# Graph attention and edge ordering: scores spread from two row halves, bf16 for zeros and ones, runs innermost and scans

## The chip, the cores and the metric

The kernel runs on one core of a Trainium2 chip. A core has a matrix engine (TensorE, PE in the profile, with its weight loads as PEld), a vector engine (VectorE, DVE), a scalar engine (ScalarE, ACT), GpSimd (POOL) and a sync engine (SP) that issues most DMAs. Each has its own instruction stream, and they wait for each other by semaphores. The metric is the device time of one execution, in microseconds (us).

## The reference

Two graph layers over 12,500 nodes and 200,000 edges sorted by destination. The change touches the first layer (attention) and the ordering of the edges that the second one (three graph convolutions) needs.

```python
h = jnp.maximum(_layernorm(x, axis=-1), 0.0)
# attention, 8 heads of 16
q, k, v = ((h @ W.T).reshape(N, 8, 16) for W in (Wq, Wk, Wv))
scores = jnp.einsum('ehc,ehc->eh', q[dst], k[src]) / np.sqrt(16) + edge_attr @ We.T
seg_max = jax.ops.segment_max(scores, dst, num_segments=N)
ex = jnp.exp(scores - seg_max[dst])
denom = jax.ops.segment_sum(ex, dst, num_segments=N)
out = jax.ops.segment_sum(v[src] * (ex / denom[dst])[:, :, None], dst, num_segments=N)
x = x + out.reshape(N, 128)
h = jnp.maximum(_layernorm(x, axis=-1), 0.0)
# three times: (h @ W)[src] * norm summed over dst, bias, ReLU, batch norm
x = x + gcn3(h)
```

## The kernel before

**Attention** (`attend`) takes the edges in 196 blocks of 1024, eight chunks of 128 lanes each. For one block GpSimd gathers the rows of k and v (`gather`, line 740, eight indirect DMAs), SyncE loads the queries and edge features. TensorE turns one-hot tables of the lanes (`hot`) and of the block's nodes (`place`) round (`turn_hot`, `turn_place`, lines 1000 and 1004), spreads the queries over the edges (`spread_q`, line 949, in two halves of the array's rows), and adds the bias (`bias`, line 1013). VectorE multiplies and adds up (`products`, `add_up`, `add_bias`); the 64 scores of a lane are turned (`turn_scores`, line 969), copied by ScalarE into `sct`, and spread over two PSUM banks (`spread_scores`, line 989, eight f32 matmuls from 64 rows, on top of a mask that `mask`, line 974, has put there). VectorE takes the two maxima (`run_max`, line 795). `near_max` (lines 926, 928, 930) brings the maxima to the nodes, `raise_max` compares with the running maximum, `scale_exp` on ScalarE makes the factor by which older sums shrink, `spread_scale` (lines 914 and 915) spreads it for the numerators and the denominators, and `shrink` and `merge` apply it on VectorE. `messages` weights v by the exponentials, `sum_up` (line 906) sums the messages by lane, and `put_nodes` (lines 937, 938) puts them to the nodes.

`steps` sets the order: each engine has a list of (lag, step). In turn i of the loop an engine does the steps of its list in that order, each on block i minus its lag. So the list is the engine's queue, and blocks i to i-4 are under way at once. The loop's body holds four turns.

**Edge ordering** (`rank`) takes 50 spans of 28 columns by 128 edges. VectorE makes a one-hot of each edge's tile (`tile_hot`, line 1651, 3584 elements), halves it by adding (`halve`, line 1659) and sums over columns in five doubling adds (`add_up`, line 1676); TensorE counts earlier equal edges (`match`, lines 1810 and 1815, with ScalarE's ReLU behind each of seven batches, then `add_ranks`). From the rank VectorE decides the slot, numbers the edges that do not fit by five more doubling adds (`run_up`, line 1702), makes one-hots of the slot's line (`line_hot`, line 1777, 28 operations) and chunk (`chunk_hot`, line 1754), loads the payload (`load_pay`, line 1763), and TensorE puts the payload down with 28 matmuls (`put_down`, line 1845). Columns are the outer dimension of these tables, the 128 lines or 29 chunks the inner one. Lags run from 0 to 4 here too, with two turns in the body.

The lines on which the order rests:

```python
for k in range(slots):
    for lag, stage in stages:
        stage(step(t * slots + (k - lag), (k - lag) % slots, t + (k - lag) // slots))
```

## Time and profile before

| | |
|---|---|
| median of 3 runs (lowest, highest) | 6932.62 us (6927.31, 6932.69) |
| the profiled execution | 6936.31 us, span 6934.5 us |
| busy share of TensorE, VectorE, ScalarE, GpSimd | 83%, 67%, 31%, 45% |
| attention, first gather to last | 219.8 to 3072.7 us |
| ordering, first to last one-hot of a tile | 3324.8 to 4010.9 us |

A busy share over the whole span mixes stages with different limits, so it is read by stage. In the rows a group is one source line on one engine; "x16" counts the instructions that a row merges, the first number is the start, the second how long the row lasts, and what stands in brackets is how long the engine was idle before it and what ended that. An f32 matmul leaves two records, a bf16 matmul or an f32 transpose one. Busy times of TensorE can touch although the engine waits a little, since the ends of its matmuls are modelled.

### The profile page before, as it was taken

To read this page: it belongs to the slowest core of one execution; us is meant where nothing else is said; L and a number is where in the kernel's file an instruction comes from. 1 tells how busy PE (TensorE), PEld (TensorE's weight loads), DVE (VectorE), ACT (ScalarE), POOL (GpSimd) and SP (SyncE) were. 2 spreads that over 40 slices of the span, in tenths; PEclk is the share of its full clock that TensorE was granted. 3 is DMA by queue.
4 is the path that set the end of the run, shared out by engine and by line. 5 is a ranking of instruction groups with operands and counts; after the bars stand their busy time and mean duration, and the time that the engine had idled before them with its cause. 6 is when DMAs were issued, how large, how long until landed. Compare 5 with 4: busy or idle time off the path is not lost. (4 is left out here: it accounts for less than half of the span.)

```text
span 6934.5 us, 161023 instructions
## 1 busy us (share of the span) xinstructions
...
## 2 busy tenths in 40 slices
...
PEclk9655555555555555555556679999999999799997
...
GB/s 145 116 89 87 88 87 88 88 88 89 87 87 87 88 89 86 89 70 131 86 66 70 65 115 105 106 103 104 102 128 104 104 105 101 163 104 106 106 102 152
DMA packets 542000, 688.39 MB, mean 99 GB/s; under 512 B 217072, under 2 KB 427905, under 8 KB 541722
## 3 DMA queue, kind: packets, MB, share of 16 engines
...
q1 hardware_dynamic: 401692, 348.45, 16.6%
...
## 5 line engine op out<-in xcount | busy, mean ns | idle before, releaser
L740 POOL DMA_INDIRECT at_kv<-kv_tab,at_idx x1568 | 1562.2, 996 | 1296.6 <-issue 593.6
L2250 ACT ACTIVATE ag_msg<-ag_pair 128x768 bf16<-128x768 f32 x1200 | 925.9, 808 | 1586.4 <-PE ag_pair L2180 1027.1
L2189 PE MATMUL ag_sum<-ag_hot,ag_msg 128*128 128x240 bf16 x10800 | 1300.5, 268 | 69.6 <-issue 55.5
L2189 PEld LDWEIGHTS ag_sum<-ag_hot,ag_msg 128*128 128x128 bf16 x10800 | 974.6, 98 | 443.3 <-issue 366.6
L2064 POOL DMA_INDIRECT ag_spill<-g_tab,ag_idx x600 | 580.1, 967 | 1429.5 <-DMA ag_idx<-spill_tab 777.8
L2119 DVE CAST ag_msg<-ag_pair 128x768 bf16<-128x768 f32 x600 | 572.9, 955 | 588.8 <-PE ag_pair L2180 277.2
L2180 PE MATMUL ag_pair<-xs,ag_pick 128*32 128x384 bf16 x14400 | 821.3, 331 | 153.4 <-DVE ag_pick L2092 63.0
L2071 POOL DMA_INDIRECT ag_spill<-g_tab,ag_idx x750 | 724.5, 966 | 462.3 <-issue 179.1
L2102 DVE TENSOR_SCALAR ag_hot<-iota_win,ag_node 128x240 bf16<-128x240 bf16 x4350 | 901.2, 290 | 0.0
L989 PE MATMUL at_ps_bc<-at_sct,at_sel_head 64*128 64x128 f32 x3136 | 696.8, 408 | 33.9 <-issue 8.2
L989 PEld LDWEIGHTS at_ps_bc<-at_sct,at_sel_head 64*128 64x128 f32 x3136 | 639.2, 308 | 52.0 <-ACT at_sct L1059 41.1
L2180 PEld LDWEIGHTS ag_pair<-xs,ag_pick 128*32 128x32 bf16 x14400 | 305.9, 95 | 476.1 <-issue 251.3
L795 DVE TENSOR_REDUCE at_ml<-at_ps_bc 128x4 f32<-128x512 f32 x392 | 267.6, 690 | 388.3 <-issue 201.4
L1810 PE MATMUL rk_t<-ar_later,ar_negi 128*128 128x512 bf16 x350 | 202.3, 578 | 179.9 <-DVE rk_oht L1651 178.6
L1073 ACT ACTIVATE at_hot_b<-at_ps_turn 128x128 bf16<-128x128 f32 x196 | 54.3, 277 | 891.4 <-PE at_ps_turn L1004 603.7
L1867 ACT ACTIVATE rk_tm<-rk_t 128x512 bf16<-128x512 f32 x350 | 208.4, 597 | 292.3 <-PE rk_t L1815 290.5
L2092 DVE TENSOR_SCALAR ag_pick<-ag_pick,iota_p 128x1024 bf16<-128x1024 bf16 x450 | 217.4, 483 | 101.9 <-DMA ag_pick<-slot_tab 94.2
L776 DVE TENSOR_TENSOR at_prod<-at_ps_q,at_kv 128x512 f32<-128x512 f32 x392 | 252.4, 686 | 48.9 <-issue 30.5
L1045 ACT ACTIVATE at_fall<-at_drop 8x128 f32<-8x128 f32 x196 | 60.5, 309 | 703.9 <-DVE at_drop L845 639.0
L949 PE MATMUL at_ps_q<-at_qd,at_hot_b 64*128 64x512 bf16 x1176 | 253.7, 558 | 12.4 <-DVE at_prod L776 7.7
L2189 PE MATMUL ag_sum<-ag_hot,ag_spill 128*128 128x240 bf16 x2250 | 256.7, 266 | 2.5 <-issue 2.4
L1777 DVE TENSOR_SCALAR rk_ohw<-ar_iota_col,rk_line_f 128x128 bf16<-128x128 bf16 x1400 | 256.4, 246 | 0.0
...
## 6 DMA issues: line engine op xcount, KB each, us to landing
...
at_attr<-attr SPq DMA_DIRECT2D x196, 128.0 KB
at_qd<-q_tab SPq DMA_DIRECT2D x1568, 12.0 KB
at_kv<-kv_tab,at_idx POOLq DMA_INDIRECT x1568
...
```

Of the source, the lines that this page charges most:

```text
L740: nc.gpsimd.indirect_dma_start(kv[:, s.slot, ch, :], None, env["kv_tab"], bass.IndirectOffsetOnAxis(ap=idx[:, s.slot, ch:ch + 1], axis=0)) ...
L795: nc.vector.tensor_reduce(ml[:, HALF * j:HALF * (j + 1)], ps_bc[j][:, :].rearrange("p (h e) -> p h e", e=P), AX.X, ALU.max).then_inc(bc_re ...
L949: last = nc.tensor.matmul(ps_q[j][:, :].rearrange("p (c d) -> p c d", d=DIM), hot_b[own, k, :], qd[own, k % 2, HALF * j:HALF * (j + 1), pa ...
L989: last = nc.tensor.matmul(ps_bc[j][:, h * P:(h + 1) * P], sel_head[:, HALF * j + h, :], sct[:, s.slot % 2, :], start=False, stop=h == HALF ...
L1777: last = nc.vector.tensor_scalar(ohw[:, s.slot, ch, :], iota_col[:, :], line_f[:, s.slot, ch:ch + 1], None, ALU.is_equal)
L2064: nc.gpsimd.indirect_dma_start(spill[:, k, o, :], None, table, bass.IndirectOffsetOnAxis(ap=idx[:, k, o:o + 1], axis=0)).then_inc(tail_in[ ...
L2071: nc.gpsimd.indirect_dma_start(spill[:, k, o, :], None, table, bass.IndirectOffsetOnAxis(ap=idx[:, k, o:o + 1], axis=0)).then_inc(spill_in ...
L2102: last = nc.vector.tensor_scalar(hot[:, k, ch, :], env["iota_win"][:, :], node[:, k, ch:ch + 1], None, ALU.is_equal)
L2119: nc.vector.tensor_copy(msg[:, p % 4, :, :], pair_ps[p % 3][:, :, 0:3 * DIM]).then_inc(copied[p], 1)
L2180: last = nc.tensor.matmul(pair_ps[p % 3][at, ch % 2, 0:3 * DIM], pick[:, k, ch * P + j * CAP:ch * P + (j + 1) * CAP], xs[:, (P // CAP) * c ...
L2189: last = nc.tensor.matmul(sum_ps[k][:, 0:WIN], row[:, part * DIM:(part + 1) * DIM], hot[:, k, ch, :], start=first and part == 0, stop=end ...
L2250: nc.scalar.activation(msg[:, p % 4, :, :], pair_ps[p % 3][:, :, 0:3 * DIM], ACT.Copy).then_inc(copied[p], 1)
```

## The change

In attention: `turn_scores` writes the 64 turned scores twice, to PSUM rows 0 to 63 and 64 to 127, with two f32 matmuls against the identity side by side; `sct` and `sel_head` get 128 rows; `spread_scores` is one step in which each head of the first bank (lower 64 rows) is followed by one of the second (upper 64 rows). The one-hot `hot`, a copy of `place` that ScalarE makes (`cast_place`), the identity, and the constants of the first two `near_max` matmuls are bf16. The turning of the two one-hots is a bf16 matmul. The matmul with `sel_aux` is gone: ScalarE makes the denominators' factor with a second exponential into `scale_d`, which `shrink` reads. TensorE sums the messages after turning the one-hots, and VectorE makes `place` and `hot` before the messages.

In the ordering: the tables `ohc`, `ohw`, `pay` have the 28 columns innermost; `line_hot` is four tensor_tensor of 32 lines by 28 columns against a constant `iota_x`; the two chains of doubling adds are each one scan; the matmuls of `put_down` read their operands with a step of 28 elements; VectorE's list is shorter and in another order.

```diff
-        sel_head = tile("sel_head", [C * HEADS, HEADS, P])
+        sel_head = tile("sel_head", [P, HALF, P])
...
-        big_c = tile("big_c", [P, HEADS, C])
-        low_row = tile("low_row", [1, HEADS * C])
-        ones_row = tile("ones_row", [1, P])
+        ident16 = tile("ident16", [P, P], BF16)
+        big_c = tile("big_c", [P, HEADS, C], BF16)
+        low_row = tile("low_row", [1, HEADS * C], BF16)
+        ones_row = tile("ones_row", [1, P], BF16)
...
-        hot = tile("hot", [P, SLOTS, P])
+        hot = tile("hot", [P, SLOTS, P], BF16)
+        place_b = tile("place_b", [P, SLOTS, P], BF16)
-        sct = tile("sct", [C * HEADS, 2, P])
+        sct = tile("sct", [P, 2, P])
...
+        scale_d = tile("scale_d", [P, P])
...
+                    dve.wait_ge(den_scale_made, s.nth)
-                    nc.vector.tensor_tensor(den, den, sa_ps, ALU.mult).then_inc(scaled, 1)
+                    nc.vector.tensor_tensor(den, den, scale_d[AUXD:AUXROWS, :], ALU.mult).then_inc(scaled, 1)
...
                     pe.wait_ge(above_made, s.nth if isinstance(s.n, int) and s.n == sh.BLOCKS - 1 else s.nth + 1)
-                    nc.tensor.matmul(sf_ps, sel_feat[:, :, :].rearrange("h d e -> h (d e)"), scale[0:HEADS, :], start=True, stop=True)
-                    nc.tensor.matmul(sa_ps, sel_aux[:, :], scale[:, :], start=True, stop=True,
-                                     tile_position=(0, AUXD)).then_inc(scale_spread, 1)
+                    nc.tensor.matmul(sf_ps, sel_feat[:, :, :].rearrange("h d e -> h (d e)"), scale[:, :], start=True,
+                                     stop=True).then_inc(scale_spread, 1)
 
                 def spread_max(s):
                     pe.wait_ge(md_made, s.nth)
...
+                    pe.wait_ge(place_cast, s.nth)
...
-                    nc.tensor.matmul(near_ps, place[:, s.slot, :], big_c[:, :, :], start=False, stop=False,
+                    nc.tensor.matmul(near_ps, place_b[:, s.slot, :], big_c[:, :, :], start=False, stop=False,
                     nc.tensor.matmul(near_ps, place[:, s.slot, :], md[:, :, :].rearrange("p c h -> p h c"),
...
-                    nc.tensor.transpose(sct_ps, sc[:, s.slot, :], ident[:, :]).then_inc(sc_turned, 1)
+                    for j in range(2):
+                        at = slice(C * HEADS * j, C * HEADS * (j + 1))
+                        last = nc.tensor.matmul(sct_ps[at, :], sc[:, s.slot, :], ident[:, :], start=True, stop=True,
+                                                tile_position=(0, C * HEADS * j))
+                    last.then_inc(sc_turned, 1)
...
-                def spread_scores(j):
-                    def run(s):
-                        pe.wait_ge(sct_made, s.nth)
-                        for h in range(HALF):
-                            last = nc.tensor.matmul(ps_bc[j][:, h * P:(h + 1) * P], sel_head[:, HALF * j + h, :],
-                                                    sct[:, s.slot % 2, :], start=False, stop=h == HALF - 1,
-                                                    skip_group_check=True)
-                        last.then_inc(bc_made[j], 1)
-                    return run
+                def spread_scores(s):
+                    pe.wait_ge(sct_made, s.nth)
+                    for h in range(HALF):
+                        for j in range(2):
+                            own = slice(C * HEADS * j, C * HEADS * (j + 1))
+                            last = nc.tensor.matmul(ps_bc[j][:, h * P:(h + 1) * P], sel_head[own, h, :],
+                                                    sct[own, s.slot % 2, :], start=False, stop=h == HALF - 1,
+                                                    skip_group_check=True, tile_position=(C * HEADS * j, 0))
+                            if h == HALF - 1:
+                                last.then_inc(bc_made[j], 1)
-                    nc.tensor.transpose(hot_ps, hot[:, s.slot, :], ident[:, :]).then_inc(hot_turned, 1)
+                    nc.tensor.matmul(hot_ps, hot[:, s.slot, :], ident16[:, :], start=True, stop=True).then_inc(hot_turned, 1)
-                    pe.wait_ge(place_made, s.nth)
-                    nc.tensor.transpose(place_ps, place[:, s.slot, :], ident[:, :]).then_inc(place_turned, 1)
+                    pe.wait_ge(place_cast, s.nth)
+                    nc.tensor.matmul(place_ps, place_b[:, s.slot, :], ident16[:, :], start=True, stop=True
+                                     ).then_inc(place_turned, 1)
...
-                    (2, spread_scores(0)), (2, spread_scores(1)), (3, sum_up), (0, turn_hot), (0, turn_place)], w)
+                    (2, spread_scores), (0, turn_hot), (0, turn_place), (3, sum_up)], w)
...
-                    nc.scalar.activation(scale[0:HEADS, :], fall[:, :], ACT.Exp, bias=env["zero_t"][0:HEADS, :],
+                    nc.scalar.activation(scale[:, :], fall[:, :], ACT.Exp, bias=env["zero_t"][0:HEADS, :],
...
+                    nc.scalar.activation(scale_d[AUXD:AUXD + HEADS, :], fall[:, :], ACT.Exp,
+                                         bias=env["zero_t"][0:HEADS, :], scale=-1.0).then_inc(den_scale_made, 1)
...
+                def cast_place(s):
+                    act.wait_ge(place_made, s.nth)
+                    nc.scalar.activation(place_b[:, s.slot, :], place[:, s.slot, :], ACT.Copy).then_inc(place_cast, 1)
+
...
-        ohc = tile("ohc", [P, SPAN_C, PLACE_C], BF16)
-        ohw = tile("ohw", [P, 2, SPAN_C, P], BF16)
-        pay = tile("pay", [P, 2, SPAN_C, PAY], BF16)
...
+        ohc = tile("ohc", [P, PLACE_C, SPAN_C], BF16)
+        ohw = tile("ohw", [P, 2, P, SPAN_C], BF16)
+        pay = tile("pay", [P, 2, PAY, SPAN_C], BF16)
...
+            nc.gpsimd.iota(iota_x[:, :, :], pattern=[[1, P], [0, SPAN_C]], base=0, channel_multiplier=0,
...
-                to = sums[0][:, PAD + 1:PAD + SPAN_C].unsqueeze(2)
-                nc.vector.tensor_tensor(to, halves[5][:, 0:SPAN_C - 1, 0:1], halves[5][:, 0:SPAN_C - 1, 1:2], ALU.add
-                                        ).then_inc(summed[0], 1)
-
-            def add_up(k):
-                def go(s):
-                    dve.wait_ge(summed[k - 1], s.nth)
-                    v, d = sums[k - 1], 1 << (k - 1)
-                    if k == 5:
-                        s.freed(dve, ranked, 2)
-                    to = before_c[:, s.slot, :] if k == 5 else sums[k][:, PAD:PAD + SPAN_C]
-                    op = nc.vector.tensor_tensor(to, v[:, PAD:PAD + SPAN_C], v[:, PAD - d:PAD - d + SPAN_C], ALU.add)
...
-                return go
+                s.freed(dve, ranked, 2)
+                nc.vector.tensor_tensor_scan(before_c[:, s.slot, 1:SPAN_C], halves[5][:, 0:SPAN_C - 1, 0],
+                                             halves[5][:, 0:SPAN_C - 1, 1], 0.0, ALU.add, ALU.add
+                                             ).then_inc(half_made, 1)
...
-            def run_up(k):
-                def go(s):
-                    dve.wait_ge(spill_made if k == 1 else run[k - 2], s.nth)
-                    v, d = spills[k - 1], 1 << (k - 1)
-                    n = SPAN_C + 1
-                    nc.vector.tensor_tensor(spills[k][:, PAD:PAD + n], v[:, PAD:PAD + n], v[:, PAD - d:PAD - d + n],
-                                            ALU.add).then_inc(run[k - 1], 1)
-                return go
+            def run_up(s):
+                dve.wait_ge(spill_made, s.nth)
+                s.freed(dve, over_made, 1)
+                nc.vector.tensor_tensor_scan(queue[:, 1:SPAN_C + 1], spills[:, :], none[:, :], 0.0, ALU.add, ALU.add
+                                             ).then_inc(queued, 1)
...
-                nc.vector.tensor_tensor(ohc[:, :, :], chunk_f[:, :].unsqueeze(2).to_broadcast([P, SPAN_C, PLACE_C]),
-                                        iota_chunk[:, :].unsqueeze(1).to_broadcast([P, SPAN_C, PLACE_C]),
-                                        ALU.is_equal).then_inc(ohc_made, 1)
+                nc.vector.tensor_tensor(ohc[:, :, :], chunk_f[:, :].unsqueeze(1).to_broadcast([P, PLACE_C, SPAN_C]),
+                                        iota_x[:, 0:PLACE_C, :], ALU.is_equal).then_inc(ohc_made, 1)
-                nc.vector.tensor_tensor(pay[:, k, :, 0:2 * PLACE_C].rearrange("p c (v m) -> p v c m", v=2),
-                                        ohc[:, :, :].unsqueeze(1).to_broadcast([P, 2, SPAN_C, PLACE_C]),
-                                        kept["vals"][:, :, here(s)].unsqueeze(3).to_broadcast(
-                                            [P, 2, SPAN_C, PLACE_C]), ALU.mult).then_inc(pay_made, 1)
...
+                nc.vector.tensor_tensor(pay[:, k, 0:2 * PLACE_C, :].rearrange("p (v m) c -> p v m c", v=2),
+                                        ohc[:, :, :].unsqueeze(1).to_broadcast([P, 2, PLACE_C, SPAN_C]),
+                                        kept["vals"][:, :, here(s)].unsqueeze(2).to_broadcast(
+                                            [P, 2, PLACE_C, SPAN_C]), ALU.mult).then_inc(pay_made, 1)
...
-                    for ch in range(q * 4, q * 4 + 4):
-                        last = nc.vector.tensor_scalar(ohw[:, s.slot, ch, :], iota_col[:, :],
-                                                       line_f[:, s.slot, ch:ch + 1], None, ALU.is_equal)
-                    if q == 6:
-                        last.then_inc(ohw_made, 1)
+                    at = slice(q * P // 4, (q + 1) * P // 4)
+                    op = nc.vector.tensor_tensor(ohw[:, s.slot, at, :], line_f[:, s.slot, :].unsqueeze(1).to_broadcast(
+                        [P, P // 4, SPAN_C]), iota_x[:, at, :], ALU.is_equal)
+                    if q == 3:
+                        op.then_inc(ohw_made, 1)
...
-                    last = nc.tensor.matmul(p_ps[k][:, 0:PAY], ohw[:, k, ch, :], pay[:, k, ch, :], start=ch == 0,
+                    last = nc.tensor.matmul(p_ps[k][:, 0:PAY], ohw[:, k, :, ch], pay[:, k, :, ch], start=ch == 0,
```

On TensorE, the middle of a turn of the attention loop before: turn_max, turn_scores, give_back, spread_scores, the sum (906), the two turns.

```order
L963 MATMUL at_ps_max<-ident,at_mnew 128x8
L966 REGISTER_ALU
L967 REGISTER_ALU
L969 MATMUL at_ps_turn<-ident,at_sc 64x128
L982 MATMUL at_ps_max<-at_m_node,at_place_t 128x8
L989 MATMUL at_ps_bc<-at_sct,at_sel_head 128x128 x8
L902 REGISTER_ALU
L906 MATMUL at_ps_node<-at_msg,at_hot_w 32x137 x8
L996 ISA
L82 REGISTER_ALU
L1000 MATMUL at_ps_turn<-ident,at_hot 128x128
L1004 MATMUL at_ps_turn<-ident,at_place 128x128
```

The same place now (999 is the spread, 911 the sum):

```order
L976 MATMUL at_ps_turn<-ident,at_sc 64x128 x2
L991 MATMUL at_ps_max<-at_m_node,at_place_t 128x8
L999 MATMUL at_ps_bc<-at_sct,at_sel_head 128x128 x8
L1006 ISA
L82 REGISTER_ALU
L1010 MATMUL at_ps_turn<-at_ident,at_hot 128x128
L1014 MATMUL at_ps_turn<-at_ident,at_place_b 128x128
L907 REGISTER_ALU
L911 MATMUL at_ps_node<-at_msg,at_hot_w 32x137 x8
L983 MATMUL at_ps_bc<-at_miss_b,at_identb 128x512 x2
```

The scores are turned by two matmuls instead of one, the spread still has eight, and the sum stands behind the two turns.

On VectorE, the end of that turn before: the bias added (789), the merge (879, 880), messages (817), short (853), hot, place, and the next turn's maxima (795).

```order
L789 TENSOR_TENSOR at_sc<-at_qk,at_ps_scale 128x64
L876 REGISTER_ALU
L879 TENSOR_TENSOR state<-state,at_ps_node 128x128
L880 TENSOR_TENSOR aux<-aux,at_ps_node 9x128
L817 TENSOR_TENSOR at_msg<-at_kv,at_msg 128x8x128
L853 TENSOR_TENSOR at_short<-at_ps_max,at_ml 128x8
L82 ISA
L758 ISA
L758 TENSOR_TENSOR at_hot<-rel,iota_w 128x128
L766 ISA
L766 TENSOR_TENSOR at_place<-off,iota_n 128x128
L795 TENSOR_REDUCE at_ml<-at_ps_bc 128x4 x2
```

And now (793 adds the bias, 821 is the messages, 799 the maxima):

```order
L884 TENSOR_TENSOR state<-state,at_ps_node 128x128
L885 TENSOR_TENSOR aux<-aux,at_ps_node 9x128
L82 ISA
L770 ISA
L770 TENSOR_TENSOR at_place<-off,iota_n 128x128
L762 ISA
L762 TENSOR_TENSOR at_hot<-rel,iota_w 128x128
L821 TENSOR_TENSOR at_msg<-at_kv,at_msg 128x8x128
L857 TENSOR_TENSOR at_short<-at_ps_max,at_ml 128x8
L799 TENSOR_REDUCE at_ml<-at_ps_bc 128x4 x2
```

`place` and `hot` moved ahead of the messages; the count of operations is the same.

On VectorE in the ordering loop before: the small tiles' halvings between adds, from the second halving to the second group of one-hot lines.

```order
L1659 TENSOR_TENSOR rk_half<-rk_half 128x896
L1702 TENSOR_TENSOR rk_spills<-rk_spills 128x29
L1659 TENSOR_TENSOR rk_half<-rk_half 128x448
L1702 TENSOR_TENSOR rk_spills<-rk_spills 128x29
L1659 TENSOR_TENSOR rk_half<-rk_half 128x224
L1702 TENSOR_TENSOR rk_spills<-rk_spills 128x29
L1659 TENSOR_TENSOR rk_half<-rk_half 128x112
L1702 TENSOR_TENSOR rk_spills<-rk_spills 128x29
L1659 TENSOR_TENSOR rk_half<-rk_half 128x56
L1708 CAST rk_spill_n<-rk_spills 128x1
L1666 TENSOR_TENSOR rk_sums<-rk_half 128x27
L1777 TENSOR_SCALAR rk_ohw<-ar_iota_col,rk_line_f 128x128 x4
```

And now, from the same halving (1783 is a quarter of the one-hot lines, 1685 the scan of the running count):

```order
L1678 TENSOR_TENSOR rk_half<-rk_half 128x896
L1715 CAST rk_spill_n<-rk_queue 128x1
L1678 TENSOR_TENSOR rk_half<-rk_half 128x448
L1783 TENSOR_TENSOR rk_ohw<-rk_line_f,rk_iota_x 128x896
L1678 TENSOR_TENSOR rk_half<-rk_half 128x224
L1678 TENSOR_TENSOR rk_half<-rk_half 128x112
L1719 TENSOR_SCALAR rk_over<-rk_queue,rk_ahead 128x28
L1678 TENSOR_TENSOR rk_half<-rk_half 128x56
L1725 TENSOR_TENSOR rk_diff<-rk_place,rk_over 128x28
L1685 SCALAR_TENSOR_TENSOR rk_before_c<-rk_half 128x27
```

The adds over spills (1702) are gone from between the halvings, where one scan (1709, ahead of these rows) does their work, and the groups of four one-hot lines have become one operation of 896 elements.

## Rows read from the trace of the kernel before

**Rows 1.** The page: busy time and share of the span; granted clock in 40 slices.
```profile
span 6934.5 us, 161023 instructions
...
PEclk9655555555555555555556679999999999799997
```

**Rows 2.** Stretches: us, busy time by engine (instructions), granted clock, DMA share, GB/s.
```profile
1000.00:2000.00 1000.00, 920.19 (x4573) 637.59 (x4571) 578.01 (x1433) 227.87 (x952) 543.33 (x546) 0.57 0.31 88
3320.00:3610.00 290.00, 189.18 (x2467) 130.91 (x2468) 276.15 (x1319) 101.85 (x221) 0.84 (x11) 0.61 0.24 72
```

**Rows 3.** Line 989: times run, ns min/median/max, first and last start.
```profile
L989 PE MATMUL at_ps_bc<-at_sct,at_sel_head x3136: 272/417/579, 237.3 to 3097.2; 64*128 64x128 f32 x196
```

**Rows 4.** TensorE in one block: start us, us, line, operation, count, idle before.
```profile
2982.80 3.78 PE L989 MATMUL at_ps_bc<-at_sct,at_sel_head 64*128 64x128 f32 x16
2986.50 1.16 PE L906 MATMUL at_ps_node<-at_msg,at_hot_w 128*32 128x137 f32 x16
...
2988.08 1.06 PE L974 MATMUL at_ps_bc<-at_miss_b,at_identb 128*128 128x512 bf16 x2
...
2989.39 0.69 PE L926 MATMUL at_ps_max<-at_low_row,at_ones_row 1*128 1x64 f32 x2
2990.00 0.69 PE L928 MATMUL at_ps_max<-at_big_c,at_place 128*128 128x64 f32 x2
2990.48 0.63 PE L930 MATMUL at_ps_max<-at_md,at_place 128*128 128x64 f32 x2
...
2991.77 0.59 PE L915 MATMUL at_ps_scale<-at_scale,at_sel_aux 9*9 9x128 f32 x2
2992.29 0.79 PE L937 MATMUL at_ps_node<-at_place,at_nodes 128*128 128x128 f32 x2
...
2993.85 1.46 PE L949 MATMUL at_ps_q<-at_qd,at_hot_b 64*128 64x512 bf16 x6
...
2996.88 0.40 PE L969 MATMUL at_ps_turn<-ident,at_sc 128*64 128x128 f32 x1 [0.37 <-DVE at_sc L789]
...
2997.71 3.78 PE L989 MATMUL at_ps_bc<-at_sct,at_sel_head 64*128 64x128 f32 x16
```

**Rows 5.** The same line 989, one block later and the next.
```profile
3012.63 3.78 PE L989 MATMUL at_ps_bc<-at_sct,at_sel_head 64*128 64x128 f32 x16
...
3024.55 2.47 PE L989 MATMUL at_ps_bc<-at_sct,at_sel_head 64*128 64x128 f32 x16 [0.18 <-ACT at_sct L1059]
```

**Rows 6.** A stretch of that block.
```profile
3020.00:3022.00 2.00, 2.00 (x14) 1.08 (x14) 1.55 (x3) 0.35 (x2) 1.34 (x2) 1.00 0.36 111
```

**Rows 7.** VectorE around the loop's edge: start us, us, line, count, idle before.
```profile
3028.75 1.29 DVE L795 TENSOR_REDUCE at_ml<-at_ps_bc 128x4 f32<-128x512 f32 x2 [2.72 <-remote]
```

**Rows 8.** The page: the gathers on GpSimd, busy us, mean ns, idle before.
```profile
L740 POOL DMA_INDIRECT at_kv<-kv_tab,at_idx x1568 | 1562.2, 996 | 1296.6 <-issue 593.6
```

**Rows 9.** VectorE in one span of the ordering stage.
```profile
3699.78 1.08 DVE L1659 TENSOR_TENSOR rk_half<-rk_oht 128x1792 bf16<-128x1792 bf16 x1
3700.78 0.18 DVE L1702 TENSOR_TENSOR rk_spills<-rk_spills 128x29 f32<-128x29 f32 x1
3700.89 0.62 DVE L1659 TENSOR_TENSOR rk_half<-rk_half 128x896 bf16<-128x896 bf16 x1
...
3702.86 0.73 DVE L1777 TENSOR_SCALAR rk_ohw<-ar_iota_col,rk_line_f 128x128 bf16<-128x128 bf16 x4
...
3708.72 0.99 DVE L1754 TENSOR_TENSOR rk_ohc<-rk_chunk_f,ar_iota_chunk 128x812 bf16<-128x812 bf16 x1
3709.93 1.85 DVE L1763 TENSOR_TENSOR rk_pay<-rk_ohc,ar_vals 128x1624 bf16<-128x1624 bf16 x1 [0.21 <-DVE rk_ohc L1754]
...
3714.00 1.08 DVE L1659 TENSOR_TENSOR rk_half<-rk_oht 128x1792 bf16<-128x1792 bf16 x1
```

**Rows 10.** TensorE in the same span.
```profile
3709.05 1.65 PE L1845 MATMUL rk_p<-rk_pay,rk_ohw 128*128 128x63 bf16 x28 [2.18 <-DVE rk_ohw L1777]
3713.21 0.61 PE L1810 MATMUL rk_t<-ar_later,ar_negi 128*128 128x512 bf16 x1 [2.51 <-DVE rk_oht L1651]
```

92 lines of the change are left out of this document (46 added, 46 removed).

## Prediction

> **What bounds the kernel now.** I read the page first, then a table by stages, then the order of time inside one turn of each loop that the change touches. One core runs for 6934.5 us, 6936.31 with what lies around the span; the median of the three runs is 6932.62, so the profiled run stands 3.7 us above it [rows 1]. The change touches two stages. Attention runs from about 220 to 3100 us in 196 blocks; the edge ordering from about 3325 to 4040 us in 50 spans. The rest (3 layers of aggregation, where the clock is high) is not touched, and I leave it at its time.
>
> In attention TensorE is busy 92% of a stretch of 1000 us, VectorE 58%, ScalarE 23%, GpSimd 54%, and the granted clock is 0.57, so it is mostly the lower level, 1.2 GHz [rows 2]. From the first to the last start of line 989, less the 3.3 us inside the last block, a block takes (3097.2 - 237.3 - 3.3) / 195 = 14.65 us [rows 3]. One block at 1.2 GHz goes from 2982.80 to 2997.71, 14.91 us, and TensorE's starts follow each other nearly without a gap: the waits there are 0.37 us for the scores and some tenths before line 989 [rows 4]. Here TensorE is the bound, and time taken out of its chain comes off the block.
>
> In the ordering the picture turns round. VectorE is busy 276.15 of 290 us, 95%, TensorE 65%, ScalarE 35% [rows 2]. A span takes 3714.00 - 3699.78 = 14.22 us [rows 9]; TensorE waits 2.18 us in it for the one-hot lines and 2.51 us for the next tile's one-hot [rows 10]. VectorE is the bound.
>
> **Attention, part by part (at 1.2 GHz).**
> (a) The spread of scores: eight f32 matmuls, 16 records, take 2986.50 - 2982.80 = 3.70 us, of which 0.35 is the change-over to the next line's tiling (16 steps of 0.21 are 3.35) [rows 4]. Each uses 64 of the 128 rows. Afterwards they go in four pairs, one of the lower half of the rows and one of the upper. Line 949 already does that, in bf16: six matmuls of 128x512 in 1.46 us. Two full-height ones of the same size (line 974) take 1.06, with one inside them 0.63 long, thus 0.43 apart; six in a row would take 5 x 0.43 + 0.63 = 2.8. So the halves there run side by side [rows 4]. If f32 does the same, 3.35 becomes 1.7 and the term is -1.65. The other bound: the f32 weights are loaded one after the other, and as 16 loads fill the 3.35 us as well as the matmuls do, nothing is gained: 0. I take -1.65, by line 949.
> (b) The matmul of line 915 goes: 2992.29 - 2991.77 = -0.52 [rows 4]. In its place ScalarE makes a second exponential and VectorE reads it from SBUF; ScalarE is at 23%.
> (c) Lines 926 and 928 become bf16, one record instead of two: now 0.61 + 0.48 = 1.09 us [rows 4]. Half is -0.5; bounds -0.2 (only the second record's step) and -0.8. The bf16 copy of place is one more ScalarE step of some 0.3 us, which TensorE meets only in turn_place, over 1.5 us later.
> (d) turn_hot and turn_place remain one record each: 0.
> (e) turn_scores (line 969, one record of 0.40) becomes two f32 matmuls side by side with two records each: one step of 0.21 more, and it lies on the path from scores to spread. +0.24.
> (f) Moving the sum behind the two transposes changes no amount of work. On VectorE place and hot now stand before the messages, so the sum's input is 0.5 us later, but the two transposes now cover that: 0.
> Sum: -1.65 - 0.52 - 0.5 + 0.24 = -2.43, about -2.5 with the gaps; 14.91 becomes 12.4.
>
> What is late next? Both halves of the spread now end together, so VectorE has its two maxima (1.29 us for two, rows 7) wholly behind it, where one lay beside the second half before. TensorE has the transposes (0.5), the sum (1.1) and the first mask (0.4) to do meanwhile: the cover is 2.0 us against 1.5, just enough. Around the edge of the loop, once in four blocks, VectorE comes 2.72 us late with these maxima [rows 7]; today the second half of the spread and the rest hide about half of that, afterwards less: +0.7 us in four blocks, 0.2 a block. GpSimd needs (1562.2 + 593.6) / 196 = 11.0 us a block for eight gathers and the gaps that nothing explains [rows 8]: a floor at 11.0, not at 12.4. VectorE has 0.58 x 14.65 = 8.5 us.
>
> The clock: the block that begins at 3012.63 takes 11.92 us (next start 3024.55), with the clock at 1.00 in a stretch of it [rows 5, 6]. It rises there right behind the sum, the transposes and the two masks. The mean of 14.65 against the cold block's 14.91 says that rises less edge stalls give 0.26 a block. That run of work stays and comes round more often, so I expect somewhat more: a net 0.5 with the edge taken off. Block: 12.4 - 0.5 = 11.9 us. Gain 2.75 x 195 = 536 us; from the bounds of (a), (c) and the clock, between 190 and 712 (the floor of 11.0).
>
> **Ordering, part by part.**
> (g) One-hot lines: 28 tensor_scalar of 128x128, four in 0.73 us, 0.65 from start to start: 7 x 0.65 = 4.55 us. Now four tensor_tensor of 128x896 bf16 with unit step inside. The row of that size, line 1659, has the next start 0.54 later when one small operation of 0.11 lies between; I take 0.54 each, 2.16. -2.4 [rows 9].
> (h) load_pay: 1.85 us for 1624 elements with a broadcast innermost; 1792 elements with unit steps take 1.08. -0.9. chunk_hot: 0.99 for 812 against 0.62 for 896. -0.4 [rows 9]. Bound for (g) and (h): if a broadcast in the middle keeps the slow rate, 1.85 us per 1624, then (g) is 4.0 and (h) nothing.
> (i) Five adds for the running count, five for the spills, 0.11 each from start to start [rows 9], become one scan each. The trace has no scan; between 0.1 and 0.5 us each for 28 elements. I take 0.2: -0.7, bounds -0.9 and -0.1.
> (j) With fewer fillers the last steps follow each other: +0.3 (line 1763 waits 0.21 on its neighbour now).
> Sum: -4.1, 14.22 becomes 10.1 on VectorE.
> (k) TensorE's put_down, 28 matmuls in 1.65 us [rows 10], now reads weights and payload with a step of 28 elements, 56 bytes. The trace has no bf16 operand so; line 930 reads f32 with a step of 32 bytes and takes 0.63 where line 928 with unit step takes 0.69 [rows 4], so at that step nothing shows beside the weight load. Line 989 streams 128 columns in 0.21 us a record, so line 930's 64 would take 0.11 and could take up to 0.21, twice as long, unseen behind its weights. Bounds: 1.65 and, if each load of 128 columns goes as slowly as f32 weights do (0.21), 28 x 0.21 = 6 us. TensorE's turn is 14.22 less its waits 2.18 and 2.51 and the some 1.1 for the spill count: 8.4 with put_down at 1.65, so it carries up to 3.3 before it binds at 10.1, and at 6 us a span takes 12.8. I take 3.3, the twofold that line 930 allows, and with the change-overs 10.5 us a span.
> The Trainium skill speaks against this part: its page "SBUF — State Buffer", section "Door 1: The DMA port swizzle", note on cachelines, says that every access which moves to another 16-byte line pays, so that bf16 is free only up to a step of 8 elements. Line 930 steps over two lines each time and shows no penalty, or one hidden behind its weights; at 28 elements no run shows it yet. By that page put_down would cost more than 1.65, by line 930 alone 1.65, and the span 10.5 or 10.1.
> Gain 3.7 x 50 = 185 us, between 70 and 230. The constants of this stage (a larger iota) are made while VectorE waits for the first load: nothing.
>
> Sum: 6936.3 - 536 - 185 = 6215, and 3.7 less against the median: 6212, say 6210.
>
> **Rivals.**
> High clock: TensorE is at 2.4 GHz so much that attention comes to GpSimd's 11.0 us. For it: block 3012.63 shows 11.92 even before the change. Against: the mean clock of 0.57 says that it falls back each time [rows 2]. 6936 - 712 - 185 = 6040.
> The halves do not overlap in f32: (a) is 0, block 13.6 us, gain 205: 6936 - 205 - 185 = 6546. Against it stands line 949, for it only that its weights are bf16.
> Ordering keeps its time: the broadcast stays slow, or the strided loads cost 6 us, gain some 70: 6330.
> Slower: changing between the row halves empties the array as changing the tiling does, 0.35 us each time. Seven changes inside the spread cost 2.45 instead of -1.65: the block is 14.91 + 2.45 - 0.78 = 16.6 or, with the clock, 16.3, +320 us; with the ordering's -185: 7070. It decides from some 0.2 us for each change. Line 949, which changes five times in 1.46 us, is against it. The Trainium skill has the same distinction: "TensorEngine Tiling (Array Packing)", section on key properties, says that changing the tiling mode drains the engine and that tiles of one mode run in parallel. By that this rival costs nothing; the 0.35 behind line 989, a change of mode, agrees.
>
> **Chances.** Both parts work, about 6210 (own range 6080 to 6350): 0.68. High clock, 6040: 0.10. No overlap, 6546: 0.07. Ordering keeps its time, 6330: 0.10. Slower, 7070: 0.05. The range 6060 to 6450 leaves out the no-overlap and slower cases and part of the high clock. A difference of 0.2% (14 us) is what can be told from none. Faster 0.94, same 0.01, slower 0.05.
>
> **What would show it.** In the changed profile: the 16 records of the spread within some 2.0 us instead of 3.78; a block at 12 us between starts; TensorE's waits in it still below 1 us, else another engine has taken over; VectorE's two maxima back to back, directly behind the spread. In the ordering: 896-element rows of some 0.6 us, the payload at 1.0, put_down's 28 matmuls in 2 to 4 us, a span at 10.5, VectorE over 90% busy. The forecast is wrong if the spread stays over 3 us, if a scan takes more than 0.5, or if TensorE waits for neither VectorE nor ScalarE in the ordering, which would mean that put_down binds.

## The result, and the profile after

The changed kernel takes 6664.91 us (6652.28 to 6674.67, 4 runs) against 6931.14: a ratio of 0.9616, interval 0.9598 to 0.9633. It is 266 us faster where 721 were forecast, and outside the forecast's range. The profiled run took 6652.28 us. In attention a block went from 14.65 to 14.18 us.

From the page of the kernel after (compare [rows 1]), then the table by stretches, whose columns are those of [rows 2]:

```profile
span 6650.5 us, 159851 instructions
...
PEclk9655555555555555555677699999999999899997
```

```profile
1000.00:2000.00 1000.00, 803.31 (x4677) 498.36 (x4673) 585.88 (x1485) 282.95 (x1133) 578.92 (x567) 0.56 0.33 91
3320.00:3610.00 290.00, 282.31 (x3418) 219.99 (x3416) 268.44 (x966) 134.40 (x315) 0.00 (x0) 0.75 0.31 91
```

The ordering did what was forecast. The 50 one-hots of a tile (line 1670 now) start within 498.4 us, 10.17 us a span; before, 3324.8 to 4010.9 makes 14.00. The line's row, and one span on VectorE and then on TensorE (answers to [rows 9, 10]):

```profile
L1670 DVE TENSOR_SCALAR rk_oht<-rk_hi_bc,iota_p x50: 1141/1144/1153, 3237.1 to 3735.5; 128x3584 bf16<-128x3584 bf16 x50
```

```profile
3508.29 0.58 DVE L1761 TENSOR_TENSOR rk_ohc<-rk_chunk_f,rk_iota_x 128x812 bf16<-128x812 bf16 x1
3509.09 1.00 DVE L1769 TENSOR_TENSOR rk_pay<-rk_ohc,ar_vals 128x1624 bf16<-128x1624 bf16 x1 [0.22 <-DVE rk_ohc L1761]
...
3511.49 0.62 DVE L1783 TENSOR_TENSOR rk_ohw<-rk_line_f,rk_iota_x 128x896 bf16<-128x896 bf16 x1
...
3513.12 0.21 DVE L1709 TENSOR_TENSOR_SCAN rk_queue<-rk_spills,rk_none 128x28 f32<-128x28 f32 x1
```

```profile
3508.91 3.43 PE L1849 MATMUL rk_p<-rk_pay,rk_ohw 128*128 128x63 bf16 x28
```

In attention TensorE's work shrank as forecast, yet it now stands idle: busy 803 of 1000 us instead of 920. The groups of TensorE in one block (answers to [rows 4]), and where VectorE waits:

```profile
1528.83 2.08 PE L999 MATMUL at_ps_bc<-at_sct,at_sel_head 64*128 64x128 f32 x16
1530.84 0.29 PE L1010 MATMUL at_ps_turn<-at_ident,at_hot 128*128 128x128 bf16 x1
1530.93 0.31 PE L1014 MATMUL at_ps_turn<-at_ident,at_place_b 128*128 128x128 bf16 x1
```

```profile
1528.01 1.02 POOL L744 DMA_INDIRECT at_kv<-kv_tab,at_idx  x1 [2.76 <-DVE aux L885]
1529.33 1.03 POOL L744 DMA_INDIRECT at_kv<-kv_tab,at_idx  x1 [0.30 <-issue]
1530.67 0.95 POOL L744 DMA_INDIRECT at_kv<-kv_tab,at_idx  x1 [0.30 <-issue]
...
1532.37 1.29 DVE L799 TENSOR_REDUCE at_ml<-at_ps_bc 128x4 f32<-128x512 f32 x2 [2.64 <-PE at_ps_bc L999]
...
1532.54 0.28 ACT L1088 ACTIVATE at_hot_b<-at_ps_turn 128x128 bf16<-128x128 f32 x1 [2.23 <-PE at_ps_turn L1014]
```

The spread is done at 1530.91, but VectorE's maxima, which need nothing else, begin at 1532.37; the two turned one-hots are done at 1531.24 and ScalarE starts on them at 1532.54. TensorE has worked, and nobody hears of it for 1.3 to 1.5 us. Three gathers started within the last 3 us. VectorE's waits over the same 1000 us (engine, waiting group, what ended the wait, us in total, times, longest):

```profile
DVE at_sc L793 <- remote: 100.0, 29, 3.6
DVE at_ml L799 <- PE at_ps_bc L999: 78.5, 38, 2.7
DVE at_mnew L848 <- remote: 33.5, 16, 2.7
```

"Remote" stands where no instruction ended shortly before the wait's end: the signal came long after its maker. The trace also holds when each semaphore was raised. Set against the ends of the matmuls that raise them (from 1000 to 2400 us), 54.5% of TensorE's updates come over 0.5 us late in the kernel after, 21% in the kernel before; of VectorE's and ScalarE's, none to speak of (0.02 and 0.03 us on average). By the number of gathers started in the 3.75 us before the end of the matmul (400 to 3000 us), over 0.3 us late are: with one 1% before and 2% after, with two 12% and 45%, with three 61% and 86%. The gathers themselves moved together: the median distance from one to the next is 1.61 us before and 1.27 after, and three in 3.75 us stand ahead of 27% of the matmuls' ends before and of 46% after (1000 to 2400 us). The trace of these runs lacks about half of all update records (of TensorE's in this stretch 21% before and 27% after); a missing one leads to the next block's, some 14 us off, which I left out. So the shares are those of the updates that were recorded.

### The profile page after: what moved, and what is told of

The parts are those of the page before. It is cut to its first block and busy times, and to the rows that moved or that the text cites. A ratio compares the mean times of both kernels' runs of the same rounds, so it can differ in the third digit from the quotient of the medians.

```text
span 6650.5 us, 159851 instructions
## 1 busy us (share of the span) xinstructions
PE 5406.7 (81%) x49582; PEld 3559.8 (54%) x49582; DVE 4418.8 (66%) x13500; ACT 2281.1 (34%) x5686; POOL 3152.5 (47%) x3144
## 3 DMA queue, kind: packets, MB, share of 16 engines
q0 software_dynamic: 140208, 338.71, 18.3%
## 5 line engine op out<-in xcount | busy, mean ns | idle before, releaser
L744 POOL DMA_INDIRECT at_kv<-kv_tab,at_idx x1568 | 1605.2, 1024 | 1169.3 <-issue 491.3
L799 DVE TENSOR_REDUCE at_ml<-at_ps_bc 128x4 f32<-128x512 f32 x392 | 252.8, 686 | 362.0 <-PE at_ps_bc L999 229.8
L999 PE MATMUL at_ps_bc<-at_sct,at_sel_head 64*128 64x128 f32 x3136 | 407.6, 438 | 11.4 <-issue 11.4
L999 PEld LDWEIGHTS at_ps_bc<-at_sct,at_sel_head 64*128 64x128 f32 x3136 | 350.0, 325 | 16.8 <-issue 12.1
L976 PE MATMUL at_ps_turn<-ident,at_sc 128*64 128x128 f32 x784 | 136.1, 440 | 242.9 <-DVE at_sc L793 227.6
L954 PE MATMUL at_ps_q<-at_qd,at_hot_b 64*128 64x512 bf16 x1176 | 283.7, 616 | 12.2 <-issue 7.1
L1024 PEld LDWEIGHTS at_ps_scale<-at_we,at_attr 128*128 128x128 f32 x784 | 181.1, 321 | 166.9 <-issue 99.3
L793 DVE TENSOR_TENSOR at_sc<-at_qk,at_ps_scale 128x64 f32<-128x64 f32 x196 | 42.6, 217 | 340.0 <-remote 281.2
L983 PE MATMUL at_ps_bc<-at_miss_b,at_identb 128*128 128x512 bf16 x392 | 194.9, 554 | 80.5 <-DVE at_ml L799 80.3
```

What stands on the lines that cost most here:

```text
L744: nc.gpsimd.indirect_dma_start(kv[:, s.slot, ch, :], None, env["kv_tab"], bass.IndirectOffsetOnAxis(ap=idx[:, s.slot, ch:ch + 1], axis=0)) ...
L799: nc.vector.tensor_reduce(ml[:, HALF * j:HALF * (j + 1)], ps_bc[j][:, :].rearrange("p (h e) -> p h e", e=P), AX.X, ALU.max).then_inc(bc_re ...
L954: last = nc.tensor.matmul(ps_q[j][:, :].rearrange("p (c d) -> p c d", d=DIM), hot_b[own, k, :], qd[own, k % 2, HALF * j:HALF * (j + 1), pa ...
L999: last = nc.tensor.matmul(ps_bc[j][:, h * P:(h + 1) * P], sel_head[own, h, :], sct[own, s.slot % 2, :], start=False, stop=h == HALF - 1, s ...
```

## The experiments

They ran in five sets, each on one chip, with the kernel before beside them. Kernels with plain loads or with half of the gathers do not compute the reference's values; all others do. The sets are of two kinds, and this turned out to be the heart of the case. In three (and in the first comparison) the kernel before took 6873 to 6931 us and TensorE's updates were late; I call them late sets. In two it took 6258 and 6264 us and no update was more than 0.30 us late; I call them prompt sets. Which kind a set would be could not be chosen, and it isn't simply the chip: the first prompt set and the first late one both ran on the chip with the number 2. Two kernels of different late sets are compared by their ratios, and the changed kernel itself had 0.9586 and 0.9616 there, so less than 0.003 between such ratios says nothing. Block is the mean time of a block in attention (the column of the late sets leaves out the first comparison).

| kernel | late sets: ratio, block | prompt sets: ratio, block |
|---|---|---|
| before | 1, 14.45 | 1, 12.5 (no trace of its own; from the last two rows) |
| after | 0.9586, 14.00 | 0.9206, 10.96 |
| ordering alone | 0.9718, 14.52 | |
| after, spread not in halves | 0.9454, 13.62 | 0.9421, 11.65 |
| after, two gates moved | 0.9519, 13.82 | 0.9196 and 0.9195, 10.97 and 11.04 |
| after, both of these | 0.9729, 14.61 | |
| after, a pause behind each gather | 0.9470, 13.66 | |
| after, plain loads for gathers | 0.8706, 10.93 | |
| after, half of them plain | 0.8680, 10.94 | |
| after, four gathers only | | 0.9156, 10.66 |
| before, one gate | 1.0937, 17.87 | 1.0006 and 1.0004, 12.52 and 12.56 |
| before, plain loads | | 0.9998, 12.54 |

**1. Half of the gathers.**

```diff
-                    for ch in range(C):
+                    for ch in range(0, C, 2):
                         pace(s, ch)
...
-                        for ch in range(HALF * j, HALF * (j + 1)):
+                        for ch in range(HALF * j, HALF * (j + 1), 2):
                             dve.wait_ge(kv_in[k][ch], 16 * s.use)
```

> The changed kernel with only four of the eight gathers of a block (chunks 0, 2, 4, 6; the rows of the other four chunks are left out, so half of the keys and values are zeros). Theory S (late signals): TensorE's semaphore updates reach the other engines 1 to 2 us late whenever GpSimd's gathers follow each other closely; in the changed kernel 45% of the updates with two gathers started in the last 3.75 us and 86% of those with three are over 0.3 us late. With half of the gathers nearly all come in time, and a block takes what TensorE's cold work needs, 12.5 us, or less, instead of 14.18: 6665 - 196 x (1.7 to 2.2), 6230 to 6330 us. Rival C (chain): with TensorE's work cut, the loop is held by a chain through VectorE and ScalarE that has nothing to do with gathers: 6640 to 6690 us. Rival K (clock): the missing gain is the clock that no longer rises; gathers do not matter for it either: 6640 to 6690 us.

It fell in a prompt set: 5725.2 us, ratio 0.9156 (0.9140 to 0.9173). Beside the changed kernel's 0.9206 in the other prompt set this says only that there four of the gathers and their data cost 0.3 us a block. The time expected was for a late set, so it decides nothing on the theory.

**2. The kernel before with one gate.** GpSimd waits ahead of each of the eight gathers for a step of VectorE (`pace`), which keeps them apart.

```diff
                 def pace(s, ch):
                     if ch == 0:
                         s.freed(pool, bc_read[0], 3)
-                    if ch == 1:
-                        s.freed(pool, md_made, 3)
...
```

> The kernel before, with seven of the eight gates in front of its gathers taken away (the first stays): the same eight gathers of a block start one behind the other. Theory S: they then stand 1.25 us apart over 10 of the 14.65 us, TensorE's signals come late as in the changed kernel, and the kernel before loses 0.5 to 1.5 us a block: 7030 to 7230 us. Rivals C and K: the gathers' places change nothing, the data only come earlier: 6920 to 6945 us.

Prompt set: 6256.97 us, 1.0006 (0.9993 to 1.0020). Repeated:

> The kernel before with only the first of its eight gates, run again because its first run fell in a set without late signals, where it changed nothing (ratio 1.0006). With late signals: the gathers stand 1.25 us apart through most of a block, over half of TensorE's updates are late, and the kernel before gets 100 to 300 us slower, ratio 1.015 to 1.045. A rival by which only the number of gathers in a block counts, and not how close they stand, has 0.997 to 1.003.

Again a prompt set: 6263.0 us, 1.0004 (0.9991 to 1.0017). And a third time:

> The kernel before with only the first of its eight gates. Its two runs so far fell in sets without late signals and changed nothing (1.0006, 1.0004). If this set has late signals: if closeness counts, more of TensorE's updates are late and it is 100 to 300 us slower, ratio 1.015 to 1.045; if only the number of gathers in a block counts, 0.997 to 1.003. Without late signals: 0.998 to 1.002 again.

This one was a late set, and the effect is over twice the most that I gave it: 7525.1 us, 1.0937 (1.0918 to 1.0955). The eight gathers in a row, and VectorE beside them:

```profile
1501.89 0.94 POOL L726 DMA_INDIRECT at_kv<-kv_tab,at_idx  x1 [8.65 <-DVE at_ml L781]
1503.14 0.95 POOL L726 DMA_INDIRECT at_kv<-kv_tab,at_idx  x1 [0.30 <-issue]
...
1510.64 0.95 POOL L726 DMA_INDIRECT at_kv<-kv_tab,at_idx  x1 [0.30 <-issue]
1519.17 0.94 POOL L726 DMA_INDIRECT at_kv<-kv_tab,at_idx  x1 [7.58 <-DVE at_ml L781]
```

```profile
1506.30 0.30 DVE L846 TENSOR_TENSOR at_nodes<-at_ps_node,at_gain 128x136 f32<-128x136 f32 x1
1510.42 0.23 DVE L810 TENSOR_REDUCE at_top_n<-at_ps_max 128x8 f32<-128x64 f32 x1 [3.81 <-remote]
```

The same work and the same number of gathers, only closer: 3.4 us more a block. Over half of the updates (56%) are over 0.5 us late, and a block that runs wholly at 1.2 GHz takes 18.3 us (median) where it takes 14.91 in a prompt set. In a prompt set the same edit does nothing. So in a late set it matters how close the gathers stand, with their number the same.

**3. Two gates moved in the kernel after.**

```diff
                     if ch == 3:
-                        s.freed(pool, near_read, 3)
+                        s.freed(pool, qk_made, 2)
                     if ch == 4:
-                        s.freed(pool, qk_made, 2)
+                        s.freed(pool, q_spread, 1)
```

The fourth gather now waits for another step of VectorE, the fifth for one of TensorE.

> The changed kernel with two gates of its gathers moved (the fourth gather waits for the sum of the products instead of the maxima at the nodes, the fifth for the queries' spread instead of the sum), so that the eight stand more evenly in a block. Theory S: fewer signals are late, but eight gathers in 12.5 us are still two to three in 3.75 us: 6520 to 6650 us. Rivals C and K: 6650 to 6680 us.

Prompt set: 5753.62 us, 0.9196 (0.9176 to 0.9217). Again, with the changed kernel beside it:

> The changed kernel with the gates of the fourth and fifth gather moved, run beside the changed kernel itself. With late signals: fewer of TensorE's updates fall behind a third gather, 20 to 150 us less than the changed kernel. Without late signals: within 20 us of the changed kernel.

Prompt set: 5764.74 us, 0.9195 (0.9176 to 0.9214), the same as the changed kernel's 5763.87. And in a late set:

> The changed kernel with the gates of the fourth and fifth gather moved. Without late signals it is the same as the changed kernel (0.9196 and 0.9195 against 0.9206). With late signals: 20 to 150 us less than the changed kernel, ratio 0.937 to 0.956; a rival by which eight gathers in a block make the same share of updates late wherever they stand has 0.956 to 0.962.

6549.42 us, 0.9519 (0.9503 to 0.9535) against the changed kernel's 0.9586 (0.9566 to 0.9606) in another late set: 36 us less by the times, 46 by the ratios. The share of late updates hardly moved (52% in both), so the share alone does not set the time. The trace shows TensorE busy 862 us of the stretch from 1000 to 2000 instead of 800, but at a clock of 0.52 instead of 0.57; which of the signals are late now was not worked out.

**4. The kernel after, as it is,** to have it in each kind of set.

> The changed kernel, unaltered. The four kernels run so far ran on another chip than the first comparison: there the kernel before takes 6258 us instead of 6931 and no semaphore update of TensorE is late in its trace, whether gathers stand close or not. Theory S' (the late signals belong to the first chip, and they are what held the change back there): on a chip without late signals the changed kernel gains more, ratio 0.91 to 0.925 (near the 0.9196 of the kernel with moved gates), on one with late signals 0.96 again. Rival: the ratio is 0.96 on every chip, and the moved gates alone brought the rest: 0.955 to 0.965.

Late set: 6585.86 us, 0.9586 (0.9566 to 0.9606).

> The changed kernel, unaltered, as the reference of this set. With late signals (the kernel before at 6870 to 6930 us): ratio 0.955 to 0.965. Without (the kernel before at some 6260): S' says 0.91 to 0.925.

Prompt set: 5763.87 us, 0.9206 (0.9191 to 0.9222), as the theory S' of the expectations had it. VectorE's waits there and the table of the stretch:

```profile
DVE at_sc L793 <- PE at_ps_scale L1024: 89.8, 82, 1.4
DVE at_ml L799 <- PE at_ps_bc L999: 67.4, 61, 1.1
```

```profile
1000.00:2000.00 1000.00, 897.31 (x6076) 565.39 (x6074) 754.84 (x1933) 363.98 (x1472) 749.49 (x737) 0.69 0.43 118
```

"Remote" is gone from the waits, no wait is over 1.4 us, and the clock is 0.69 instead of 0.56, although gathers start every 1.25 us.

**5. The kernel before, for its trace.**

> The kernel before, unaltered, for its trace beside the others. S': where it takes some 6260 us, no update of TensorE is late, cold blocks still take 14.9 us, and the clock is at 2.4 GHz for more than half of the blocks; where it takes some 6930, about a fifth of the updates is late.

Late set, 6865.95 us; 18% of the updates over 0.5 us late.

**6. The ordering alone.** `attend` as before, `rank` as after.

> Only the part of the change in the edge ordering; attention as before. A span went from 14.22 to 10.2 us in the first traces, so 50 x 4.0 = 200 us less whatever the chip: 6931 - 200 = 6730 or 6258 - 200 = 6058 us, ratio 0.968 to 0.971. A rival by which the faster ordering is given back elsewhere (code loading, the constants) has less than 150 us.

6676.23 us, 0.9718 (0.9699 to 0.9738): 197 us. In that set attention's part of the change is worth 6676 - 6586 = 90 us.

**7. Plain loads for gathers, in the kernel after.**

```diff
-                        nc.gpsimd.indirect_dma_start(
-                            kv[:, s.slot, ch, :], None, env["kv_tab"],
-                            bass.IndirectOffsetOnAxis(ap=idx[:, s.slot, ch:ch + 1], axis=0)
-                        ).then_inc(kv_in[s.slot][ch], 16)
+                        nc.gpsimd.dma_start(kv[:, s.slot, ch, :], env["kv_tab"][P * ch:P * (ch + 1), :]
+                                            ).then_inc(kv_in[s.slot][ch], 16)
```

> The changed kernel with the eight gathers of a block replaced by eight plain loads of the same bytes (128 rows of kv_tab in a row each, the same ones in every block; the data are not the edges'), issued by GpSimd at the same gates. On a chip with late signals: if it is the gather's work of making 128 descriptors that delays TensorE's signals, they come in time and the time falls by 350 us or more against the changed kernel; if it is the bytes, it stays within 50 us. On a chip without late signals: GpSimd issues faster, so if GpSimd's 11.0 us are what a block waits for it falls by up to 60 us, else it stays within 20 us of the changed kernel.

Late set, beside experiment 4's first run: 5977.33 us, 0.8706 (0.8682 to 0.8729), 608 us below the changed kernel. The page's line on DMA has the same packets and bytes in both (115 GB/s is of this shorter run, 105 of the other); below it the stretch from 1000 to 2000 us, where the changed kernel has TensorE at 800 us and a clock of 0.57:

```profile
DMA packets 541998, 688.37 MB, mean 115 GB/s; under 512 B 217072, under 2 KB 427905, under 8 KB 541722
```

```profile
1000.00:2000.00 1000.00, 897.07 (x6053) 565.91 (x6053) 750.19 (x1922) 363.02 (x1468) 392.87 (x733) 0.69 0.40 118
```

No update is late, and a block takes 10.93 us, what it takes with gathers in a prompt set. So the number of packets and bytes does not delay TensorE's signals; it goes with the gather (0.95 us of GpSimd each, against 0.54 for a plain load). One rival is left: the plain loads read the same 1024 rows in every block, the gathers scattered ones, and no run parts GpSimd's work from the addresses.

**8. The same in the kernel before.**

> The kernel before with the eight gathers of a block replaced by plain loads of the same bytes by GpSimd, as in the run of the changed kernel with plain loads (that took 5977 us where the changed kernel took 6586 and the kernel before 6873). Theory S: the late signals cost the kernel before as well, since with them the clock rises less often; without them a block goes from 14.5 to about 11.65, as in the set where the kernel before took 6258. If this set has late signals: 6873 - 196 x 2.8 = 6320, range 6250 to 6400, ratio 0.91 to 0.93; attention's part of the change is then worth 6320 - 5977 - 197 = 146 us, with a range of 70 to 230 by the range of the time, and not the 536 of the forecast. Rival: the late signals were brought in by the change; the kernel before stays within 60 us of itself.

Prompt set, where there is nothing to mend: 6262.43 us, 0.9998 (0.9985 to 1.0011). A late set was not to be had for it.

**9. The spread not in halves, all else as after.** `turn_scores`, `sct`, `sel_head` and `spread_scores` as in the kernel before.

> The changed kernel with the spread of the scores undone: one transpose of the scores, and eight f32 matmuls one after the other from 64 rows; all else as changed. The trace of the changed kernel shows the spread at 2.08 us instead of 3.78, so TensorE gets 1.4 us more to do in a block (1.65 less the 0.24 of the turned scores). Theory S: that work fills time in which TensorE waits for late signals, and the gathers stand wider apart; a block goes from 14.18 to 14.2 to 14.6 us: 6665 to 6750 us. Rival K or a TensorE-bound loop: the 1.4 us come back in full: 6900 to 6950 us.

Prompt set: 5888.36 us, 0.9421 (0.9402 to 0.9441).

> The changed kernel with the spread of the scores undone. Without late signals it took 5888 us, 124 more than the changed kernel (5764 in the next set), 0.69 us of a block. With late signals: TensorE's 1.4 us more lie in time in which it waits for its own signals' effect, so it is 0 to 80 us slower than the changed kernel's ratio of 0.9586: 0.958 to 0.971.

Late set: 6505.3 us, 0.9454 (0.9439 to 0.9470). My range began above it: without the row halves the kernel is faster than with them, by 81 us or, by the ratios, 91. Its gathers stand wider apart (median 1.47 us against 1.27), its trace has only 7% of the updates over 0.5 us late, and "remote" is nearly gone:

```profile
DVE at_sc L790 <- PE at_ps_scale L1016: 90.4, 65, 1.5
...
DVE at_above L812 <- remote: 14.6, 5, 4.2
```

And yet a block takes 13.62 us where it takes 11.65 in the prompt set. The same stretch in the late set, then in the prompt one:

```profile
1000.00:2000.00 1000.00, 930.97 (x4659) 644.98 (x4658) 625.08 (x1550) 295.23 (x1181) 614.75 (x592) 0.53 0.34 95
1000.00:2000.00 1000.00, 923.76 (x5582) 628.96 (x5580) 747.52 (x1859) 346.99 (x1417) 705.96 (x710) 0.70 0.40 114
```

TensorE is as busy, but the clock is 0.53 instead of 0.70. A block wholly at 1.2 GHz takes 13.4 us in both sets; of 185 blocks 154 are such in the late set and 68 in the prompt one. This kernel loses by the clock's missing rises and hardly by waits.

**10. Four gathers and four plain loads.**

> The changed kernel with four of the eight gathers (chunks 1, 3, 5, 7) replaced by plain loads of the same bytes at the same gates (their data are not the edges'). With late signals: two gathers then seldom stand within 3.75 us with a third, under a tenth of TensorE's updates is late, and a block takes nearly the 10.93 us of eight plain loads: ratio 0.87 to 0.885. If the number of gathers counts and not their distance, half of the gain comes: 0.91 to 0.92. Without late signals: as the changed kernel, 0.918 to 0.922.

Late set: 5973.94 us, 0.8680 (0.8666 to 0.8694). Four gathers left, and the whole loss is gone, not half of it: they start 2.4 us apart (median), and 5% of the updates are over 0.5 us late.

**11. A pause behind each gather.**

```diff
                         ).then_inc(kv_in[s.slot][ch], 16)
+                        if ch or not (isinstance(s.n, int) and s.n < 1):
+                            pool.wait_ge(paused, C * (s.nth - 1) + ch)
+                            alone(pool)
+                        nc.gpsimd.memset(pause[:, :], 0.0).then_inc(paused, 1)
```

> The changed kernel with a memset of 128x192 on GpSimd behind each gather, so that two gathers start at least some 1.6 us apart instead of 1.25, 12.8 us a block. With late signals: if each gather keeps TensorE's signals back for about 1.5 us and what comes faster piles up (an estimate from the shares of late updates: 0.24 before, 0.57 after, by the gathers' distances in those traces), under a tenth is late now and a block goes from 14.0 to 12.8 or 13.2: 6586 - 160 to 240 = 6350 to 6430, ratio 0.923 to 0.935. If distance is not the cause, the pauses only cost: 6600 to 6900, 0.96 or more. Without late signals: GpSimd is the bound at 12.8 us a block, 1.8 more than 10.96: 5764 + 355 = 6120, ratio 0.97 to 0.985.

Late set: 6513.81 us, 0.9470 (0.9454 to 0.9485). Better than without, against the rival, but 72 us and not the 160 to 240 that I expected. The trace shows that the pause was shorter than planned, and gathers still start 1.39 us apart:

```profile
1507.57 0.27 POOL L752 MEMSET at_pause<- 128x192 f32 x1
1508.00 0.95 POOL L745 DMA_INDIRECT at_kv<-kv_tab,at_idx  x1 [0.16 <-POOL at_pause L752]
1508.95 0.28 POOL L752 MEMSET at_pause<- 128x192 f32 x1
1509.39 0.95 POOL L745 DMA_INDIRECT at_kv<-kv_tab,at_idx  x1 [0.17 <-issue]
```

39% of the updates are late instead of 52%. The step from 1.25 to 1.39 us brought 0.34 us a block although GpSimd got more to do; that 1.6 would bring the rest was not tried.

**12. No row halves and the moved gates.**

> The changed kernel without row halves in the spread and with the two gates moved. With late signals (0.9454 and 0.9519 with one of the two edits each, 0.9586 with none): if they add up 0.939; if the gates were only of use while many signals are late, 0.943 to 0.947. Without late signals: as the kernel without row halves, 0.941 to 0.943.

Late set: 6693.97 us, 0.9729 (0.9713 to 0.9745). Neither: each edit helps alone, together they cost 189 us against the first of them. 33% of the updates are late, the gathers stand 1.37 us apart (median) instead of 1.47, and a block takes 14.61 us; TensorE is at 1.2 GHz nearly throughout (clock 0.50 from 1000 to 2000 us). A gate that suits one order of the work bunches the gathers in another; I can't forecast which.

## Why the prediction was wrong

**The step that failed** is the first of attention: "Here TensorE is the bound, and time taken out of its chain comes off the block." The amounts were right within some 0.5 us a block. The spread went from 3.78 to 2.08 us (forecast -1.65), line 915 went, lines 931 and 933 take 0.17 us from the first to line 935 where 1.09 stood (forecast -0.5, more than the bound of 0.8), the turned scores stand 0.6 us before the next line where 0.2 stood (forecast +0.24). A block without late signals at 1.2 GHz takes 11.98 us in the prompt set, where the sum said 12.4. But in a late set what was taken from TensorE came back as waits for its own signals: a block wholly at 1.2 GHz takes 15.1 to 15.3 us there (median; 14.9 before the change). The loop got shorter, the gathers moved together (median distance 1.61 to 1.27 us), and the share of late updates rose from 21 to 54%. Of the 2.75 us a block of the forecast some 0.45 came. That late signals hold the block is shown by the plain loads beside it (experiment 7); that the gathers moved together because their gates did is argued.

**The row that showed it** is [rows 7]: 2.72 us <-remote ahead of the two maxima. I read it as the loop's edge, once in four blocks, and gave it 0.2 us. It is a late signal: the spread's two matmuls that signal end at 3025.59 and 3026.91, and their updates are recorded at 3028.62 and 3028.71, with gathers starting 1.2 to 1.6 us apart from 3018.12 to 3026.45. Nor is it the loop's edge: over all blocks the waits of more than 2 us ahead of line 795 fall 8, 7, 7 and 8 times on the four turns of the loop's body. I had no rival for it. The kernel before already loses by late signals, 12.5 us a block in a prompt set and 14.45 in a late one, but not as the change does: a block wholly at 1.2 GHz takes 14.9 us in both. What it loses is the clock, which is at 2.4 GHz for 246 of the 1900 us from 300 to 2200 in the late set (experiment 5) and for 567 in the prompt one (one gate).

**The clock.** I expected more rises. In the late sets it is 0.56 to 0.57 in both kernels, and lower in some variants (0.53 without row halves, 0.50 in experiment 12). It is not the set by itself that keeps it down: with plain loads in the same late set it is 0.69. Why 7% of late updates are enough to keep it at 0.53 stays open. In the prompt set it is 0.69 against 0.65 in the kernel before with one gate. There attention's part is worth 12.54 - 10.97 = 1.57 us a block, some 305 us, and not 536: the clock is at 2.4 GHz for three tenths of the time already before, and there the same work is worth less (the spread takes 2.47 us with the clock mostly at 2.4 GHz and 3.78 at 1.2, [rows 4, 5]).

**GpSimd's floor** of 11.0 us was a rival's end. In a prompt set a block takes 10.97 us, with plain loads 10.93 and with four gathers 10.66, so it costs at most some 0.3 us.

**The ordering** was right by its sum, with luck in one term: 14.00 to 10.17 us a span, forecast 10.5, 197 us alone where 185 were forecast. Its terms: one-hot lines 0.62 each (4 in place of 28 small ones), payload 1.00, chunk 0.58, a scan 0.21 us (I took 0.2 within 0.1 to 0.5). put_down takes 3.43 us for 28 matmuls where 1.65 stood, near the 3.3 taken. But the 1.65 is at 1.2 GHz and the 3.43 of the row at 2.4: before, the 28 took 1.04 us in the 15 spans where the clock was at 2.4 GHz, and after they take 3.4 us at either level. The step of 56 bytes thus costs the twofold against the one and over the threefold against the other, so that the twofold came out right is luck. The Trainium skill's page "SBUF — State Buffer", section "Door 1: The DMA port swizzle", note on cachelines, speaks for such a cost and the trace agrees, while the bound from line 930 was too kind. TensorE is now busy 282 of the 290 us and waits only for ScalarE, 0.25 us a span; VectorE is busy 268 and waits 0.6 us in every second span for the spill count, which comes by way of TensorE. So both are at their limit, and no run says which sets the 10.17.

**Elsewhere.** The three layers of aggregation gather too. From their first to their last sum (lines 2189 and 2193) they take 2714 us in the late set and 2485 in the prompt one, for the kernel before and after alike (2748 in the first comparison; the 34 more are not explained). There 46 to 49% of TensorE's updates are over 0.5 us late in the late sets and none in the prompt ones. So between the two kinds of set the kernel before differs by some 375 us in attention and 230 there, and the changed one by 590 and 230. That the 230 come from the late signals too is argued: no run had plain loads in that stage.

The forecast of 6210 holds for no set: where signals are late the gain is 266 to 287 us, where they are prompt 500, from a kernel before that takes 6264 there.

**What would serve.** Of the kernels that compute the reference, the one without row halves (0.9454) and the one with a pause (0.9470; the intervals overlap) are the fastest in late sets, the kernel after (0.9206) in prompt ones, together with the moved gates. The kernel with moved gates is better or the same in both (0.9519 and 0.9195 against 0.9586 and 0.9206), and so is the one to keep where the kind of set can't be chosen. In the late sets it did not run beside the changed kernel. The pause has no run in a prompt set.
